# A state-space scan that reads PSUM directly, block by block, and value projections written to both partition halves by four narrow matmuls

## The reference, cut to what matters

```python
qkv = x @ Wqkv
q, k, v = jnp.split(qkv, 3, -1)
...
attn = jax.nn.softmax(sim, -1)
out = jnp.einsum('bhwij,bhwje->bhwie', attn, bv2)
```

```python
def step(h, inp):
    d_t, x_t, B_t, C_t = inp
    A_bar = jnp.exp(d_t[:, :, None] * A)
    h = A_bar * h + (d_t * x_t)[:, :, None] * B_t[:, None, :]
    y_t = jnp.einsum('bdn,bn->bd', h, C_t)
    return (h, y_t)
```

## Time and profile before

| what | value |
|---|---|
| runs | 2736.12 and 2733.21 us, median 2734.66 us |
| the profiled execution's own time | 2734.42 us |
| its span | 2732.6 us |
| mean granted TensorE clock | 0.948 of full speed |
| TensorE matmul busy | 2391.9 us (88%) |
| VectorE busy | 2401.9 us (88%) |
| ScalarE busy | 1988.0 us (73%) |
| GpSimd busy | 1164.5 us (43%) |

### The profile page before, as it was taken

The page is one execution under the profiler, slowest core; times in us unless marked ns, Lnnn a source line. Parts: engine busy times, 40 slices in busy tenths (PEclk is TensorE's granted clock), DMA queues, the critical chain, the costliest instruction groups (busy, mean ns, idle before and its releaser), DMA issues. The chain is left out here.

```text
span 2732.6 us, 60708 instructions
## 1 busy us (share of the span) xinstructions
PE 2391.9 (88%) x23660; PEld 1246.6 (46%) x23660; DVE 2401.9 (88%) x2594; ACT 1988.0 (73%) x3169; POOL 1164.5 (43%) x465
## 2 busy tenths in 40 slices
PE   7789999999999999999999999999998765565778
PEld 2345555555555555555555555555554222122355
DVE  5799999999999999999999999999995799999542
ACT  4778888888888888888888888888886643333433
POOL 0444444444444444444444444444441066566130
PEclk8899999999999999999999999999999877678889
DMA  0100000000000000000000000000000100000001
GB/s 20 52 2 2 2 24 10 10 2 2 24 10 10 2 13 13 9 10 2 13 13 14 5 2 13 13 17 2 2 2 1 36 0 0 0 0 0 17 16 46
DMA packets 15995, 29.49 MB, mean 11 GB/s; under 512 B 3616, under 2 KB 6064, under 8 KB 15664
## 3 DMA queue, kind: packets, MB, share of 16 engines
q1 hardware_dynamic: 15760, 25.78, 3.0%
HBM read 24.73 MB, written 1.05 MB: 9 GB/s over the span
## 5 line engine op out<-in xcount | busy, mean ns | idle before, releaser
L705 POOL TENSOR_TENSOR f_rot<-f_raw,f_tabc 128x1024 f32<-128x1024 f32 x192 | 453.0, 2360 | 925.3 <-DVE f_qk L753 583.6
L709 POOL TENSOR_TENSOR f_rot<-f_rot,f_shuf 128x1024 f32<-128x1024 f32 x192 | 452.4, 2356 | 235.6 <-DVE f_shuf L746 235.6
L746 DVE TENSOR_TENSOR f_shuf<-f_shuf,f_tabs 128x1024 f32<-128x1024 f32 x192 | 427.9, 2229 | 8.6
L776 DVE TENSOR_TENSOR f_s<-f_s,f_rcp 128x512 f32<-128x512 f32 x192 | 401.5, 2091 | 6.6
L604 ACT ACTIVATE f_raw<-f_ps 128x1024 f32<-128x1024 f32 x192 | 196.0, 1021 | 227.3 <-PE f_ps L425 227.3
L472 PEld LDWEIGHTS f_ps<-f_ptz,f_v 64*64 64x64 f32 x6144 | 259.1, 133 | 146.9 <-issue 146.9
L1133 POOL TENSOR_TENSOR s_prod<-s_state,s_cs 128x1024 f32<-128x1024 f32 x64 | 234.1, 3677 | 169.4 <-DVE s_state L1211 142.3
L968 PE MATMUL s_ps<-s_prod,s_ident 128*128 128x512 f32 x256 | 183.0, 872 | 132.7 <-POOL s_prod L1133 132.7
L595 ACT ACTIVATE f_v<-f_ps 64x256 f32<-64x256 f32 x768 | 287.0, 374 | 6.7
L472 PE MATMUL f_ps<-f_ptz,f_v 64*64 64x96 f32 (+1 forms) x6144 | 285.4, 243 | 2.3 <-ACT f_ptz L625 2.3
L424 PE MATMUL f_ps<-f_xs,f_wq 128*128 128x512 f32 x384 | 211.8, 633 | 71.1 <-ACT f_rn L613 47.1
(11 more groups left out here) (266 smaller groups left out, 3961.3 us busy)
## 6 DMA issues: line engine op xcount, KB each, us to landing
e_w<-in_e_w SPq DMA_DIRECT2D x16, 256.0 KB, 2.8
f_wq<-in_f_wq SPq DMA_DIRECT2D x12, 256.0 KB, 2.6
f_wk<-in_f_wk SPq DMA_DIRECT2D x12, 256.0 KB, 3.4
f_wv<-in_f_wv SPq DMA_DIRECT2D x12, 256.0 KB, 3.6
f_wo<-in_f_wo SPq DMA_DIRECT2D x6, 512.0 KB, 3.3
f_w<-in_f_w SPq DMA_DIRECT2D x6, 341.0 KB, 2.9
s_dx<-in_k_pick SPq DMA_DIRECT2D x1, 1536.0 KB, 9.1
f_w<-in_f_w SPq DMA_DIRECT2D x6, 192.0 KB, 3.2
```

The costliest lines, as they stand in the source:

```text
L705: pool.tensor_tensor(view(rot, 0, [S, 4], [1, S]), view(raw, 0, [S, 4], [1, S]), view(tab_c, 0, [S, 2], [0, 2], [1, S]), ALU.mult).then_in ...
L709: pool.tensor_tensor(rot[:, :], rot[:, :], shuf[:, :], ALU.add).then_inc(sem["rot"], 1)
L746: dve.tensor_tensor(view(shuf, 0, [S, 4], [1, S]), view(shuf, 0, [S, 4], [1, S]), view(tab_s, 0, [S, 2], [0, 2], [1, S]), ALU.mult).then_i ...
L776: dve.tensor_tensor(view(t, 0, [64, 8], [1, 64]), view(t, 0, [64, 8], [1, 64]), view(rc, 0, [1, 8], [0, 64]), ALU.mult).then_inc(sem["p"], 1)
```

## The change

In the attention, the one value matmul becomes four, each with 64 tokens as the stationary side and 256 value columns (four runs of 64) as the moving one: r picks the tokens, h picks the heads and the half of the output partitions. The PSUM bank then already has the layout of v, and one ScalarE copy of 128 x 512 takes the place of four.

In the state-space layer the order becomes half, group, state: four blocks (h, k) of 16 steps, 64 steps in all. VectorE reads B of a step straight from PSUM (banks 4 and 5), and its scan reads the decay from PSUM (banks 2 and 3), where ScalarE writes it; B is no longer copied, and there is one decay buffer in place of four. C is copied as before, now once per step instead of once per state, and B and C are spread by TensorE once per step. The sums use banks 0 and 1. Each block's product with the gate (`gated`) stands between the drive and the scan of the second step of the next block. `soft(1)` stands behind block 0 on ScalarE, `split(3)` behind block 0 and `drives(1)` behind block 1 on VectorE. The zero columns are set by VectorE in PSUM.

```diff
@@ values(i, q), TensorE
-                pe.matmul(bank(2), xs[:, 128 * (q % 4):128 * (q % 4) + 128], wv[:, CH * (q // 4):CH * (q // 4) + CH],
-                          start=True, stop=True).then_inc(sem["v_mm"], 1)
+                for r in range(2):
+                    for h in range(2):
+                        at = 128 * (q % 4) + 64 * r
+                        mm = pe.matmul(view(ps, 2 * CH + 256 * r, [1, 256], p0=64 * h, rows=64), xs[:, at:at + 64],
+                                       view(wv, CH * (q // 4) + 64 * h, [128, 4], [1, 64]),
+                                       start=(r == 0), stop=True, skip_group_check=True)
+                mm.then_inc(sem["v_mm"], 1)
@@ value_copy(i, q), ScalarE
-                for r in range(2):
-                    for h in range(2):
-                        ins = act.activation(view(v, (2 * (q % 4) + r) * CH + 256 * (q // 4), [64, 4], [1, 64], p0=64 * h, rows=64),
-                                             view(ps, 2 * CH + 64 * h, [128, 4], [1, 64], p0=64 * r, rows=64), ACT.Copy)
-                ins.then_inc(sem["v"], 1)
+                act.activation(view(v, 2 * (q % 4) * CH + 256 * (q // 4), [CH, 2], [1, 256]),
+                               view(ps, 2 * CH, [256, 2], [1, 256]), ACT.Copy).then_inc(sem["v"], 1)
@@ state_space, TensorE
+            def spread(h, i, n):
+                need(pe, sem["drive"], i)
+                for c in range(2):
+                    mm = pe.matmul(bank(BB + c), pick[:, bass.ds(n * C, C)],
+                                   parts[:, h * H + c * CH:h * H + c * CH + CH], start=True, stop=True)
+                mm.then_inc(sem["b_mm"], 1)
+                need(pe, sem["c_in"], i)
+                for c in range(2):
+                    mm = pe.matmul(bank(CB + c), pick[:, bass.ds((n + DS) * C, C)],
+                                   parts[:, h * H + c * CH:h * H + c * CH + CH], start=True, stop=True)
+                mm.then_inc(sem["c_mm"], 1)
+            def add(i, par, first=False):
+                pe.wait_ge(sem["prod"], i + 1)
+                for c in range(2):
+                    mm = pe.matmul(bank(YB + c), ident[:, :], prod[par][:, c * CH:c * CH + CH],
+                                   start=first, stop=True, skip_group_check=True)
+                mm.then_inc(sem["acc"], 1)
...
+                with pe.Fori(1, DS // 2 - 1) as n2:
+                    for par in range(2):
+                        spread(h, n2 * 2 + (base + par + 1), n2 * 2 + (par + 1))
+                        add(n2 * 2 + (base + par - 1), 1 - par)
@@ state_space, ScalarE
+            def step(h, k, i, n, par):
+                need(act, sem["scan"], i)
+                act.activation(view(ps, DB * CH + 1, [S, B // 2], [1, S - 1]),
+                               view(delta, k * T + h * H + 1, [S, B // 2], [1, S - 1]),
+                               ACT.Exp, scale=aneg[:, bass.ds(n, 1)]).then_inc(sem["decay"], 1)
+                act.wait_ge(sem["c_mm"], i + 1)
+                need(act, sem["prod"], i - 1)
+                act.activation(view(cs[par], 0, [1, H]), view(ps, CB * CH, [1, H]), ACT.Copy).then_inc(sem["c_in"], 1)
@@ state_space, GpSimd
-            for par in range(2):
-                for k in range(K):
-                    zero = pool.memset(view(decay[par][k], 0, [S, B // 2], [1, 1]), 0.0)
-            zero.then_inc(sem["zero"], 1)
...
+            def step(i, par):
+                pool.wait_ge(sem["scan"], i + 1)
+                pool.wait_ge(sem["c_in"], i + 1)
+                need(pool, sem["acc"], i - 1)
+                pool.tensor_tensor(prod[par][:, :], st[par][:, :], cs[par][:, :], ALU.mult).then_inc(sem["prod"], 1)
@@ state_space, VectorE
+            dve.wait_ge(sem["dpre"], 2 * NCH)
+            dve.memset(view(ps, DB * CH, [S, B // 2], [1, 1]), 0.0).then_inc(sem["zero"], 1)
+            dve.wait_ge(sem["zero"], 1)
+            def drive(h, k, i, par):
+                dve.wait_ge(sem["b_mm"], i + 1)
+                need(dve, sem["prod"], i - 1)
+                dve.tensor_tensor(st[par][:, :], dx[:, k * T + h * H:k * T + h * H + H], view(ps, BB * CH, [1, H]),
+                                  ALU.mult).then_inc(sem["drive"], 1)
+            def scan(i, par):
+                dve.wait_ge(sem["drive"], i + 1)
+                dve.wait_ge(sem["decay"], i + 1)
+                dve.tensor_tensor_scan(st[par][:, :], view(ps, DB * CH, [1, H]), st[par][:, :], 0.0, ALU.mult,
+                                       ALU.add).then_inc(sem["scan"], 1)
...
+            for b, (h, k) in enumerate(BLOCKS):
+                base = b * DS
+                drive(h, k, base, 0)
+                scan(base, 0)
+                drive(h, k, base + 1, 1)
+                if b:
+                    gated(b - 1)
+                scan(base + 1, 1)
+                with dve.Fori(1, DS // 2) as n2:
+                    for par in range(2):
+                        drive(h, k, n2 * 2 + (base + par), par)
+                        scan(n2 * 2 + (base + par), par)
+                if b == 0:
+                    split(3)
+                if b == 1:
+                    drives(1)
+            centre(0)
+            centre(1)
+            gated(len(BLOCKS) - 1)
```

More of the change, by code:

```diff
@@ L883, in state_space @@
         pick = m.mem.enter_context(nc.sbuf_tensor("s_pick", [96, 2 * DS * C], BF16))
[L885 to L887 removed]
+        st, prod, cs = ([m.sb(f"s_{n}{par}", T // 2) for par in range(2)] for n in ("state", "prod", "cs"))
         ident = m.sb("s_ident", C)
@@ L902, in state_space @@
         added = m.sem("s_added")
-        D0, D1 = 2 * K, 2
+        BLOCKS = [(h, k) for h in range(2) for k in range(K)]
+        YB, DB, BB, CB = 0, 2, 4, 6
         body = ExitStack()
@@ L1199, in _, with gated @@
             split(2)
[L1201 to L1212 removed]
+            dve.wait_ge(sem["dpre"], 2 * NCH)
[11 more added lines that the diff above has]
+                                       ALU.add).then_inc(sem["scan"], 1)
+            def gated(b):
+                h, k = BLOCKS[b]
+                a = slice(k * T + h * H, k * T + h * H + H)
+                dve.wait_ge(sem["acc"], (b + 1) * DS)
+                dve.tensor_tensor(ysum[:, a], gate[:, a], view(ps, YB * CH, [1, H]), ALU.mult).then_inc(sem["gated"], 1)
             def centre(c):
```

132 lines of the change are left out of this document (36 added, 96 removed).

## The result

The changed kernel takes 2694.56 us (2693.53 and 2695.59), the kernel before 2734.66: a ratio of 0.9853, 95% interval 0.9811 to 0.9896, so 1.5% faster and inside the 2% that count as no change. The forecast was 2604 us, 91 us too low, and the measured time lies 30 us above the upper end of the range, 2665 us.

The account below looks back on a forecast made before the run. VectorE, held by GpSimd's products, was taken to bound the scan stage, TensorE and ScalarE to set the attention's pace. From 2734.4 us, 108 (scan stage) and 22 (values) came off: 2604 us, range 2560 to 2665.

Parts of the forecast that it names:

- The scan: Scan stage: scans 3.6 us apart, the stage 248.7 us where it took 354.3, a gain of 108 us.
- two SBUF inputs and GpSimd's product exclude each other: Scan stage: a drive or scan with two SBUF inputs can't run beside GpSimd's product; VectorE stands about 2 us per drive.
- rival 3: Scan stage: the clock stays at half, period 5.0 us, 90 us more, 2694 us; chance 0.07.
- Side by side or not: Attention's value matmuls: two column tiles run side by side in the same 0.86 us; otherwise 0.86 us more for each.
- Rival 4: Attention: the 128 x 64 tiles don't run side by side; slower, 2763 us, up to 2830; chance 0.08.
- switch of tiling: TensorE in the attention: each change of tiling costs, 0.15 to 0.3 us each slot, 1.4 us a unit.
- Net 0.95 us a unit, over 23 units 22 us: Attention: what the new values gain at the end, switching paid; bounds 83 us gained to 38 us lost.
- the projection of slot 7 then 1.25 us earlier ... so VectorE's wait for L512 shrinks by 1.25: Attention: earlier matmuls from slot 5 on bring slot 7's projection forward, cutting VectorE's 1.6 us wait by 1.25 us.
- two instructions overlap: Scan stage, drive's time: two instructions start 0.08 us before the one ahead ends, so the drive ends some 1.15 us after the scan.
- the 2.8 us of waits in rival 4: Attention: waits a unit that the slower value matmuls would fill, taken off their 8.5 us a unit.
- Rival 2: Attention gains nothing, switching takes what ScalarE gives: 2626 us, down to 2664 with 38 lost; chance 0.13.
- units over 84 us: Attention: sign that the prediction is wrong, joined to value matmuls of 1.7 us; expected were units of about 82.6 us.

Follow-up runs that it names:

- e9: e5b with the decay written to a tile in SBUF and read there by the scan, waits and single buffer kept; 2687.50 us, ratio 0.9823.
- e5b: The changed kernel with 34 one-column matmuls (136 instructions) added on TensorE ahead of the attention's loop; 2624.23 us, ratio 0.9607 to the kernel before.
- e8b: e5b with VectorE writing the next unit's input xs in slot 5 ahead of soft_b instead of behind it; 2616.12 us, ratio 0.9573.
- e11: The changed kernel with the ten value matmuls ahead of the loop in their old form, no filler, and xs written early; 2613.31 us, ratio 0.9558.
- e4: The kernel before with 120 idle instructions (waits long satisfied) on TensorE ahead of the attention's loop; 2807.77 us, ratio 1.0263.
- e6b: The changed kernel with 26 one-column matmuls (104 instructions) on TensorE ahead of the attention's loop; 2717.92 us, ratio 0.9955.
- e7b: The changed kernel with 54 one-column matmuls (216 instructions) on TensorE ahead of the attention's loop; 2635.95 us, ratio 0.9645.
- e10: The changed kernel with 64 small matmuls (256 instructions, a whole block) on TensorE ahead of the attention's loop; 2697.84 us, ratio 0.9853.

## Why the prediction was wrong, point by point

**The scan: right.** Drive 1.20 (1.2), product 2.37 (2.2 to 2.4), scan 2.29 (2.27), period 3.62 (3.6), stage 250.8 (248.7), everything behind the attention 107.5 us less (108). Its reason, that two SBUF inputs and GpSimd's product exclude each other, is shown for the scan: give it two SBUF inputs again and it is held until the product ends (3.21 to 3.27 us in e9). No run gives the drive its second SBUF input back; its 1.20 us in place of 3.20 fit the same reason. The clock in the stage came back from 0.76 to 0.95, against rival 3; the forecast had 1.00. Two bf16 matmuls of the spread take 0.60 us there (L957 at 2325.37), each 0.38 by itself, so they start 0.22 us apart, as the working took. Windows of the stage, the kernel before and the changed one:

```profile
2184.11:2538.39 354.28, 212.96 (x378) 75.42 (x378) 353.31 (x142) 133.19 (x129) 229.68 (x63) 0.76 0.00 0
```

```profile
2252.35:2503.16 250.81, 190.09 (x504) 64.75 (x505) 233.05 (x143) 134.28 (x131) 149.38 (x63) 0.95 0.00 0
```

**Side by side or not: right.** The eight instructions of the four narrow matmuls start 1.02 us ahead of what follows, here in the changed kernel:

```profile
1020.97 1.08 PE L417 MATMUL f_ps<-f_wv,f_xs 128*64 128x256 f32 x8
1021.99 1.12 PE L429 MATMUL f_ps<-f_xs,f_wq 128*128 128x512 f32 x2
```

One after another they would take 1.72 (8 x 256 columns at 0.43 us for 512). The old form took 0.95 (L414 to L472 in the earlier trace rows). Rival 4 falls. For the switch of tiling the trace of before shows, besides the 0.09 us, weights of L414 that start 0.43 us ahead of their pass (1019.41 and 1019.84) and those of L472 that start only with its first matmul (1020.79); what the working put on that, 0.05 to 0.1 us, was an estimate.

**"Net 0.95 us a unit, over 23 units 22 us": wrong twice.** The step that failed first is the sum of the values itself: it held only durations of instructions, switches of tiling and waits between engines, and put where the code lies at nothing, without a word. It left out that 12 more instructions per value, 120 ahead of the loop, move the loop's start in the code. That is worth 2042.5 - 1965.5 = 77 us in the attention's stretch, the difference of the changed kernel and e5b, 3.2 us a unit. Two hints of it were there before and were passed over, 218 packets of instructions in the page of before and the restart gap of 0.4 us by "issue" in its waits, though neither says where a block ends. The four units above split it. Two units of e5b, without a gap:

```profile
1074.29:1157.15 82.86, 80.01 (x983) 43.62 (x982) 78.22 (x91) 62.19 (x91) 37.74 (x16) 1.00 0.03 9
1240.38:1323.05 82.67, 80.01 (x983) 43.62 (x982) 78.25 (x91) 62.17 (x91) 37.77 (x16) 1.00 0.01 2
```

With the clock at 1.00 a unit of the changed kernel takes 84.3 to 85.0 us, 1.6 to 2.2 us more than these 82.8: that is the gap. With the clock at 0.98 and 0.96 they take 86.6 and 88.1: another 2 and 3.5 us for passes at half clock. (1 - 0.96) x 88.06 / 0.5 = 7 us at the lower level, 0.50, in which matmuls take about twice their time (0.83 us a pass in the earlier trace rows, 0.43 in the earlier trace rows), give 3.5. Over the whole stretch the trace's clock records put 88.7 us of the changed kernel at the lower level and 6.8 of e5b. Half of the difference, 41 us, and the 34.8 us of the gaps make 76 of the 77. That the gap brings on the lower clock is shown by its coming and going with it: 68 to 99 us at the lower level in the five runs with the gap, 3 to 10 in the nine without. In the changed kernel it falls in the gap or up to 1.7 us behind it in 16 of 21 turns; why not in the others isn't shown.

Second, the gain itself was sized too high. e5b's stretch is 7.1 us shorter than before, 0.3 us a unit in place of 0.95. The step that failed here is "the projection of slot 7 then 1.25 us earlier ... so VectorE's wait for L512 shrinks by 1.25": it shrank by 0.6 (1.6 to 1.0). Between slot 5 and slot 7 stands slot 6, where the next unit's first projection waits for xs, and xs is the last thing that VectorE does in slot 5. What TensorE is ahead there, it waits: 1.1 us. I followed TensorE's line past an edge from VectorE that had no wait before, because TensorE came later. e8b gives 0.44 of it back. Adding both, the attention gains 0.74 a unit (1972.6 - 1955.0 = 17.6 us). The remaining 0.2 is less than what VectorE lost by the move: its idle time is 30.6 us lower than before (120.9 to 90.3, 1.3 a unit), but it is busy 13.0 us longer (1851.7 to 1864.7), 0.5 a unit.

**The sum.** Of the steps of the working one is inexact, at no cost: two instructions overlap by 0.09 us in the earlier trace rows, not 0.08. And the 2.8 us of waits in rival 4 are 2.3 in the earlier trace rows; the other 0.5 is a wait of L424 for the gelu L637 that the rows don't show. Forecast -108 and -22; measured -107.5, -7.1 for the values themselves and +77 for the place of the loop: -37.6, and the two profiled spans differ by 38.8 (the first shuffle came 1.2 us earlier). With the values at 7 and the place kept, the forecast would have been 2734.4 - 108 - 7 = 2619 us; e5b is 2624 us, and its filler delays the first shuffle by 4.5 (91.2 against 86.7).

**The rivals.** Rival 2 ("gains nothing", 2626 to 2664) was nearest in size for what the values are worth by themselves. Rival 3's 2694 us is the measured number, by chance: it came from a clock at half in the scan stage, which ran at 0.95. The working named units over 84 us as a sign of being wrong; they came (84.3 to 88.1), but not with the value matmuls of 1.7 us that it joined to them (1.02). None of the rivals had the mechanism that decided.

## What to carry to other kernels

Ahead of costing a change in or ahead of a loop, count instructions too: where a loop's code is fetched anew in each turn (here ten packets of 16.4 KB a unit), instructions added or taken ahead of it move its start against the blocks in which code comes. Here that gave or took 3.6 to 4.7% of the attention's stretch with nothing else changed. A gap by "issue" in the middle of a run of equal instructions, once per turn, is its mark; shift the loop's start by some tens of instructions (here a different form for the peeled part did it without filler, e11) until long instructions stand between the restart and the block's end. When an engine is freed, look at every edge into it, also at those that show no wait now, and when VectorE's work is moved, look at what GpSimd does at the new place (here the write of xs went from 0.29 to 0.80 us in the mean).

## What the runs showed of the hardware that was not expected

- The same loop, with not one instruction in it changed, takes 3.6 and 4.7% more of the attention's stretch by where it starts: 1972.6 against 2043.1 us (before and e4), 1965.5 against 2057.3 (e5b and e6b).
- From the restart of the loop to the score matmul behind the gap pass 2.6 to 3.2 us in the four turns shown, wherever the block ends. At 10 instructions from the end the gap is 2.2 us in the mean of 21 turns (46.8 us), at 114 it is 1.7 (34.8): the 52 scores between, 0.6 us of work, cover just 0.6 us of the fetch.
- VectorE's write of 64 x 255 elements with a single SBUF input takes 0.29 us on average in e5b. In e8b, where half of them stand beside a GpSimd product, it is 0.80, and such a pair took 2.55 us.
- A filler matmul of one column is not free: with weights of 128 columns 68 passes took 9.43 us in e5b (0.14 each, granted clock 0.80) and 108 took 20.70 in e7b (0.19 each, clock 0.56). With 32 columns of weights and 8 streamed, 128 passes took 5.04 us in e10 (0.04 each, clock 0.79).
